# Feed-forward's second product with 512 tokens moving, and another order of units in the attention

## The reference

```python
x = x + attention(layernorm(x))     # 16 heads of 16, softmax over 512 keys
x = x + ffn(layernorm(x))           # out = fwht(silu(x @ W1.T) * (x @ W3.T)) @ W2.T, hidden size 1024
x = x + memory(layernorm(x))        # gated store, scan with decay 0.95 over the tokens, gated load, product
x = x + ffn(layernorm(x))           # the same feed-forward again
```

## Time and profile before

| | us |
|---|---|
| median of 3 runs (564.72 to 565.11) | 565.0 |
| the profiled execution | 566.53 |
| its span | 564.7 |
| PE busy | 552.5 (98%) |
| PEld busy | 383.0 (68%) |
| DVE busy | 382.9 (68%) |
| ACT busy | 311.8 (55%) |
| POOL busy | 178.4 (32%) |

### The profile page before, as it was taken

One profiled execution on the slowest core, in us unless ns is written; L12 is line 12 of the kernel. 1 busy time (PEld: TensorE's weight loads), 2 busy tenths in 40 slices (PEclk: granted clock), 3 DMA queues, 4 the chain that ended last, 5 costly groups with the idle time before them and its releaser, 6 DMA issues.

```text
span 564.7 us, 8930 instructions
## 1 busy us (share of the span) xinstructions
PE 552.5 (98%) x3220; PEld 383.0 (68%) x3220; DVE 382.9 (68%) x729; ACT 311.8 (55%) x581; POOL 178.4 (32%) x209
## 2 busy tenths in 40 slices
PE   8999999999999998999999999999999999999997
PEld 4543343344434433468888888888888888988887
DVE  6988888898898899836465545746886437363333
ACT  3668889876987797743233223366775333323231
POOL 5794467562546242520202002233332010100100
PEclk9989999999999999999999999999999999999999
DMA  7354540231023030021001020110000210112101
GB/s 231 100 180 146 168 132 3 68 128 34 3 94 133 6 147 3 2 74 25 15 7 31 1 38 2 21 18 1 0 2 1 37 39 15 23 38 38 38 1 37
DMA packets 48443, 29.41 MB, mean 52 GB/s; under 512 B 33496, under 2 KB 41688, under 8 KB 48016
## 3 DMA queue, kind: packets, MB, share of 16 engines
q1 hardware_dynamic: 47180, 27.77, 17.1%
q10 hardware_dynamic: 1220, 1.07, 0.7%
HBM read 10.89 MB, written 5.24 MB: 29 GB/s over the span
## 4 chain that ended last, share of the span: by engine, by line
PE 91%; DVE 4%; ACT 2%; issue 1%; DMA 1%; ACTq 0%; POOL 0%; SPq 0%; POOLq 0%
PE PS L392 89%; DVE mxr L1096 2%; PE PS L403 1%; ACT PR L921 1%; PE PS L590 1%; DMA ring<-mT 1%; DMA X<-in_x 1%; DVE OT L1161 0%; ACTq L883 0%; DVE X L1265 0%; DVE X L1178 0%; ACTq L907 0%; DVE bst L1050 0%; PE PS L527 0%; POOL rstd L1338 0%
## 5 line engine op out<-in xcount | busy, mean ns | idle before, releaser
L392 PE MATMUL PS<-xTh,ring 128*128 128x512 f32 x608 | 188.1, 391 | 0.0
L1096 DVE TENSOR_REDUCE mxr<-PS 128x1 f32<-128x512 f32 x256 | 162.9, 680 | 25.5 <-PE PS L392 24.6
L921 ACT ACTIVATE PR<-PS 128x512 f32<-128x512 f32 x256 | 138.0, 602 | 30.3 <-PE PS L392 29.9
L392 PEld LDWEIGHTS PS<-xTh,ring 128*128 128x128 f32 x608 | 113.2, 188 | 23.7 <-issue 1.7
L392 PE MATMUL PS<-xTl,ring 128*128 128x512 f32 x304 | 110.1, 391 | 0.0
L793 ACT ACTIVATE AOh<-PR 128x512 fp32r<-128x512 f32 x72 | 45.5, 632 | 111.4 <-DVE PR L1235 105.9
L392 PE MATMUL PS<-ring 50*128 50x512 f32 (+1 forms) x512 | 100.0, 454 | 4.4 <-DVE mxr L1096 2.8
L1342 POOL TENSOR_TENSOR xTl<-xf,xTh 128x512 fp32r<-128x512 f32 x30 | 42.4, 1428 | 164.9 <-ACT xTh L793 164.9
L1235 DVE TENSOR_TENSOR PR<-PR,PS 128x512 f32<-128x512 f32 x64 | 43.4, 678 | 71.9 <-PE PS L392 51.8
L392 PEld LDWEIGHTS PS<-ring 50*128 50x128 f32 (+1 forms) x512 | 41.6, 185 | 71.1 <-ACT PR L921 43.2
L1088 DVE TENSOR_TENSOR AOl<-PR,AOh 128x512 fp32r<-128x512 f32 x72 | 51.0, 709 | 45.5 <-ACT AOh L793 45.4
(11 more groups left out here) (134 smaller groups left out, 623.6 us busy)
## 6 DMA issues: line engine op xcount, KB each, us to landing
ring<-qh SPq DMA_DIRECT2D x48, 128.0 KB, 2.8
xf<-PR SPq DMA_DIRECT2D x112, 32.0 KB, 1.9
ring<-ql SPq DMA_DIRECT2D x24, 128.0 KB, 2.8
ring<-weight_scratch SPq DMA_DIRECT2D x3, 1024.0 KB, 4.8
weight_scratch<-in_w SPq DMA_DIRECT2D x2, 1024.0 KB, 6.8
X<-in_x SPq DMA_DIRECT2D x3, 512.0 KB, 4.7
out<-X SPq DMA_DIRECT2D x6, 256.0 KB, 2.2
X<-in_w SPq DMA_DIRECT2D x1, 1024.0 KB, 5.5
```

Source lines behind the costliest of these rows:

```text
L392: return nc.tensor.matmul(dst, lhsT, rhs, start=start, stop=stop, skip_group_check=True)
L921: nc.scalar.activation(PR[:, j % 8, :], PS[:, kq_bank(j), :], ACT.Exp, scale=HD ** -0.5)\
L1096: nc.vector.tensor_reduce(mxr[:, S % 2, blk, TT * p + t:TT * p + t + 1], PS[:, QK0 + i % 3, :], AX.X, ALU.max, negate=True).then_inc(max_d ...
```

## The change

1. `down(f)` has a second form for the six chunks of `TURNED = (0, 1, 2, 8, 9, 10)`: the 128 x 128 block of `W2` is stationary and all 512 tokens of the hidden tile move. That is 2 x 3 = 6 matmuls of 512 columns in place of 12 of 256. The result has features in the partitions. So DVE turns the two banks in 32 x 32 blocks into `qf` (`turn_output`), SP puts the blocks in place with 16 DMAs (`output_blocks`, into the idle half of `Vp`), and POOL adds them to `X` (`add_turned`). Chunks 3 and 11 keep the old form; the waits on `x_done` follow, as do the places of the output's stores on SP.
2. The second half of the output projection changes places with the second half of the value projection (`OUT_AT`, `V_AT`), which moves its addition on DVE from step 27 to step 31, and the rounding of the first `AOf` of a batch from ACT's step 28 and POOL's step 29 to step 31 and to step 5 of the next batch.
3. In the last batch the output projection of batch 2 moves from steps 20, 24 and 26 to steps 8, 10, 12 and 14, the last turn of maxima from step 19 to step 20 (behind that step's scores), the split of `W_LIN` from steps 23 to 26 to steps 26 to 29, and the rounding of `AOf` to steps 21 and 22.

```diff
-OUT_AT = ((20,), (24, 26))
-V_AT = ((22,), (28, 30))
-MAX_AT = 3
+OUT_AT = ((20,), (28, 30))
+V_AT = ((22,), (24, 26))
+LAST_OUT_AT = ((8, 10), (12, 14))
+MAX_AT, LAST_MAX_AT = 3, 20
+AO_AT, LAST_AO_AT = STEPS - 1, 21
+TURNED = (0, 1, 2, 8, 9, 10)
...
+            def output_blocks(n):
+                i = TURNED.index(n)
+                sp.wait_ge(y_turned, 2 * i + 2)
+                if i:
+                    sp.wait_ge(x_done, 2 * (TURNED[i - 1] + BATCH + 1))
+                for a in range(4):
+                    for c in range(4):
+                        sp.dma_start(*output_block(a, c)).then_inc(y_in, DMA)
...
             for n in range(BATCH):
                 turned_blocks(n + BATCH + 1)
+                if n in TURNED:
+                    output_blocks(n)
...
 # turn_maxima, PE
                 if s // 8 == 0:
                     pe.wait_ge(x_f, 2 * (b + 1))
-                elif s // 8 < 3 and b < BATCH - 1:
+                elif b == BATCH - 1:
+                    pe.wait_ge(x_done, 2 * b - 2 + s // 8)
+                elif s // 8 < 3:
                     pe.wait_ge(qk_f, 4 * b + 2 * (s // 8))
-                elif s // 8 == 3:
-                    pe.wait_ge(*((x_done, 2 * b) if b else (w2h_done, 3)))
+                else:
+                    pe.wait_ge(*((v_copied, 2 * b + 4) if b else (w2h_done, 3)))
...
 # shared_bank, PE
-                    pe.wait_ge(*((v_copied, 2 * b + 2) if b > 1 else (w2h_done, 4)))
+                    pe.wait_ge(*((x_done, 2 * b - 2) if b > 1 else (w2h_done, 4)))
                     ln_transpose(0, MB)
...
 # down(f), PE
+                    if f == 0 and n - 1 in TURNED:
+                        pe.wait_ge(y_turned, 2 * TURNED.index(n - 1) + 2)
...
+                    if n in TURNED:
+                        for d in range(KD):
+                            ds_ = slice(d * P, (d + 1) * P)
+                            last_ = split_mm(PS[:, 4 + d, :], [(W2l[:, f, ds_], W2h[:, f, ds_], AOl[:, f % 4, :],
+                                                               AOh[:, f % 4, :])], f == 0, f == FT - 1)
+                            if f == FT - 1:
+                                last_.then_inc(y_ready, 1)
+                        return
...
 # ACT's step
-                if s == OUT_AT[1][-1] + 2:
+                if s == (LAST_AO_AT if b == BATCH - 1 else AO_AT):
                     act.wait_ge(aof_ready, 2 * b + 1)
...
 # DVE
-                if b == BATCH - 1 and SPLIT_AT <= s < SPLIT_AT + 8:
-                    w_split_hi((s - SPLIT_AT) // 4, (s - SPLIT_AT) % 4)
+                if b == BATCH - 1:
+                    for w, at in ((W_UP, SPLIT_AT), (W_LIN, 26)):
+                        if at <= s < at + 4:
+                            w_split_hi(w, s - at)
...
+            def turn_output(n):
+                i = TURNED.index(n)
+                if i:
+                    dve.wait_ge(y_in, 16 * DMA * i)
+                for d in range(KD):
+                    dve.wait_ge(y_ready, 2 * n + d + 1)
+                    nc.vector.transpose(qf[:, d, :], PS[:, 4 + d, :]).then_inc(y_turned, 1)
...
 # POOL's step
+                if s == 5 and b:
+                    output_lo(2 * b - 1)
                 if s == 6 and b:
                     output_lo(2 * b)
-                if s == OUT_AT[1][-1] + 3:
+                if s == LAST_AO_AT + 1 and b == BATCH - 1:
                     output_lo(2 * b + 1)
...
+            def add_turned(n):
+                c = n % BATCH
+                pool.wait_ge(y_in, 16 * DMA * (TURNED.index(n) + 1))
+                for k in range(KD):
+                    v = X[:, TT * c:TT * c + TT, k * P:(k + 1) * P]
+                    y = output_sum()[:, k * SEQ:(k + 1) * SEQ].rearrange("p (t u) -> p t u", u=P)
+                    nc.gpsimd.tensor_tensor(v, v, y, ALU.add).then_inc(x_done, 1)
```

More of the change, by code:

```diff
@@ L262, in max_copy, with out_at, turned_at @@
             return ring[r:r + 2, b % 2, QI, 2 * g:2 * g + 2, :].bitcast(F32), mT[16 * blk:16 * blk + 16, :]
+        def out_at(b):
+            return LAST_OUT_AT if b == BATCH - 1 else OUT_AT
+        def turned_at(K):
+            S = (K + LEAD) // 8 - 1
+            if S == LAST_GROUP - 1:
+                return S if K % STEPS == LAST_MAX_AT else None
+            return S if K % 8 == MAX_AT and S < LAST_GROUP else None
         block = ctx.enter_context(nc.Block())
@@ L352, in _ @@
                         weights_in(W_LIN)
[L353 to L356, removed]
+                    S = turned_at(STEPS * b + s)
+                    if S is not None:
+                        max_rows(S)
                     if b == 0 and s == 24:
@@ L376, in _, with store @@
                 turned_blocks(n + BATCH + 1)
+                if n in TURNED:
+                    output_blocks(n)
             ov = out.rearrange("b (t p) d -> b p t d", p=P)
+            def store(c):
+                n = 1 if c == BATCH - 1 else 2
+                for t in range(0, TT, n):
+                    sp.wait_ge(x_done, 2 * (3 * BATCH + c) + (t // n + 1 if n == 1 else 2))
+                    sp.dma_start(ov[c, :, t:t + n, :], X[:, c * TT + t:c * TT + t + n, :]).then_inc(out_done, DMA)
             for c in range(BATCH):
-                n = 1 if c == BATCH - 1 else 2
                 if c < BATCH - 1:
                     turned_blocks(3 * BATCH + 1 + c)
-                for t in range(0, TT, n):
-                    sp.wait_ge(x_done, 2 * (3 * BATCH + c) + t // n + 1)
-                    sp.dma_start(ov[c, :, t:t + n, :], X[:, c * TT + t:c * TT + t + n, :]).then_inc(out_done, DMA)
+                if c:
+                    store(c - 1)
+                if c < BATCH - 1:
+                    output_blocks(2 * BATCH + c)
+            store(BATCH - 1)
             sp.wait_ge(out_done, (2 * BATCH + 2) * DMA)
@@ L624, in shared_bank @@
                         .then_inc(had_ready, 1)
[L625 to L633, removed]
+                for half in range(2):
+                    at = out_at(b)[half]
+                    if b and s in at:
+                        if s == at[0]:
+                            pe.wait_ge(aol_done, 2 * b)
+                            pe.wait_ge(mt_ready, turned)
+                        for part in range(2) if len(at) == 1 else (at.index(s),):
+                            out_projection(half, part)
                 if s == V_AT[0][0] and more:
@@ L659, in _ @@
                     weigh_values((K - 3) // 2)
-                S = (K + LEAD) // 8 - 1
-                if s % 8 == MAX_AT and S < LAST_GROUP:
+                S = turned_at(K)
+                if S is not None:
                     turn_maxima(S, b, s)
@@ L962, in _ @@
                             qk_split(b + 1, n)
-                if s % 8 == MAX_AT and (K + LEAD) // 8 - 1 < LAST_GROUP:
-                    max_evacuate((K + LEAD) // 8 - 1)
+                S = turned_at(K)
+                if S is not None:
+                    max_evacuate(S)
             act.wait_ge(aof_ready, 2 * BATCH)
```

32 lines of the change are left out of this document (24 added, 8 removed).

## The result

| | before | after |
|---|---|---|
| median of the runs, us | 564.86 (564.48 to 565.11) | 569.82 (568.69 to 571.53) |
| ratio after to before | | 1.0078, 95% interval 1.0048 to 1.0108 |
| profiled execution, us (span) | 566.53 (564.7) | 568.69 (566.9) |
| mean granted clock, profiled execution | 0.997 | 0.991 |
| mean granted clock, four runs of after | | 0.991, 0.988, 0.988, 0.985 |

The change makes the kernel 0.8% slower. The forecast was 563.4 with a range of 559.0 to 566.8; all runs of after lie above it. The page says at once that something is new on TensorE: the busy time has hardly moved though 288 matmuls have gone, and the 16th slice (213 to 227 us) has less than the full clock, where before has a 9 from the fourth slice on the earlier trace rows.

The account below looks back on a forecast made before the run. PE was taken to bound both feed-forward rounds and batches 1 and 2, DVE then ACT and PE the last batch. Terms -4.7 + 2.6 + 0.5 = -1.6 on 566.53 gave 564.9, median forecast 563.4, range 559.0 to 566.8 us.

Parts of the forecast that it names:

- The last batch, steps 4 to 18: Batch 3: DVE's wait for POOL delays PE's step 8 by 1.9; with longer pairs the last maximum comes 3.7 us later.
- my rivals: Three alternatives: no wait at step 4 (0.15), last batch's end not shrinking (0.14), second product gaining nothing (0.09).
- The product with 512 tokens: Feed-forward, six chunks: six 512-column matmuls replace twelve of 256 per hidden tile, saving 4.7 us at 0.2265 each.
- third rival: Feed-forward second product gains nothing, 12 short matmuls costing what 6 long ones do; median 568.1, chance 0.09.
- The way back: Feed-forward: DVE's transposes, SP's 16 extra DMAs a chunk and POOL's additions fit beside PE; cost 0.
- Step 4: Batches 1 and 2: DVE's turn into AOf waits 2.0 us for POOL, PE loses 1.6 in each.
- Step 27: Batches 1 and 2: the turn of maxima no longer waits for DVE's output addition, gaining 0.3 in each.
- The last batch, +3.7: Batch 3: the last maximum comes 1.9 + 1.8 = 3.7 us later, from the wait and the longer pairs.
- Behind the last maximum: Last batch, last maximum to last exp: shorter by 2.8 or 3.8 us, middle 3.2 taken.
- second rival: The last batch's stretch behind the last maximum stays 16.8 us, not shrinking; median 566.6, chance 0.14.
- Sum: Whole kernel: -4.7 + 2.6 + 0.5 = -1.6 us on the profiled 566.53, giving 564.9, or 563.4 as median.

Follow-up runs that it names:

- e4: After plus six 128x512 products that nobody reads, added on TensorE at step 5 of batches 1 to 3; 564.9 us.
- e2: Before with the feed-forward part of the change alone; 561.0 us.
- e8: e1 with the last batch put back to before's order (output products, last turn of maxima, rounding); 561.5 us, 560.5 at full clock.
- e3: Before with the attention part of the change alone; 572.9 us.
- e9: Before with one edit: GpSimd forms the rest of AOf's earlier half at step 5 of the next batch, not step 29 of its own; 579.6 us.
- e5: After with GpSimd's rest of AOf's earlier half at step 0, not step 5, in batch 3 alone; 564.8 us.
- e6: After with GpSimd's rest of AOf's earlier half at step 0, not step 5, in batches 1 and 2 alone; 564.9 us.
- e1: After with GpSimd's rest of AOf's earlier half at step 0, not step 5, in batches 1 to 3; 560.7 us.
- e7: e1 with ScalarE's last silu and its rounding placed before the scaling of XNs in chunk 3; 561.5 us.
- e10: After plus three 128x512 products that nobody reads, added on TensorE at step 5 of batches 1 to 3; 567.3 us.

## Why the prediction was wrong

**The step that failed** stands in "The last batch, steps 4 to 18": "PE's step 8 comes 1.9 later", and with it the 1.6 each of batches 1 and 2. That wait itself, its cause, its place and its releaser were right. Its price was taken as a shift of the work behind it at the clock of the earlier trace rows, "granted in full". The price has a second part: PE stands, and behind a stand of that length the clock falls to its lower level. In the profiled execution this is 3.3 us, and e4 shows that it goes when PE is given something to do. All that the clock costs the four runs of after is 4 to 7 us (0.985 to 0.991); that holds falls without a stand too, as the one from 22 to 26 us in the profiled run, and how much of it lies behind stands in the other three no trace shows. None of my rivals had this, so the range ended at 566.8. The trace of before did hold a hint: its clock falls once, near 40 us, which is the one slice with an 8 in the earlier trace rows, and the run of 566.53 lies 1.5 above the median, which is about that fall's price (0.003 of clock, 1.4). I used the 1.5 as a mere offset.

Point by point:

- **The product with 512 tokens, -4.7.** Right. 0.2265 a matmul throughout, 32.64 a chunk, 6 x 0.76 = 4.6. The third rival falls, for both measured forms kept their distances. The Trainium skill's "TensorE: Matmul & The Clock Gate", "Back-to-back issue gap", does not agree with these rows: by its 2.5 ns per matmul the six chunks would have gained 0.7, and they gained 4.6. The Trainium skill's section calls that formula the gap of an isolated matmul, which the prediction left out, and gives about 131 ns for 512 columns in a sustained stream; the rows have 226.5. e2 has the half at 3.9, near 4.6 less chunk 3's 0.4.
- **The way back, cost 0.** Nearly right. The SP queue has the room that I worked out (351.34 + 10.38 = 361.7 against a call at 364.10). ACT still waits 0.60 for the last block and chunk 3 loses 0.4. I have not shown why that block lands late.
- **Step 4, 1.6 in each of batches 1 and 2.** The mechanism was right, the size low: 2.06 and 1.79. PE stands 1.71 and 1.52, near my 1.6. Nearly all of the rest is lost in the same pair of steps: in batch 1 it takes 102.80 - 97.59 = 5.21 us against 100.75 - 97.53 = 3.22 before, 1.99 more. The idle time of a row counts from the end of the matmul before it, which in a stream overlaps the next, so the stand's figure is less than what PE loses.
- **Step 27, -0.3 each.** Right: 0.27 and 0.29.
- **The last batch, +3.7.** The wait of 1.9 was 1.92. The pairs cost some 1.7 against 1.8.
- **Behind the last maximum, -3.2.** 13.0 in place of 13.6: a gain of 3.9 by ACT's own row of work, the upper end (3.8) of what I had worked out, not its middle. With e8's 1.9 for both together the second rival falls.
- **Sum.** Shifts of all terms as measured give about -1.2, my -1.6 was 0.4 off; at full clock the runs have -0.3. The forecast of 563.4 lies 1.1 below the 564.5 of after at full clock; the other 5.3 of the miss of 6.4 us are the clock, with falls behind the stands and falls without one.

## What to carry to other kernels

When a change lets TensorE stand for a microsecond or two in a stretch that was unbroken, the stand's length is the lower end of its price; look for a lower granted clock behind it, and put that price in the range. An instruction of an engine with half its time free can still be the dearest of the change by its place in the order: ask which in-order engine waits for it, and what else that engine has queued. Before reading a difference of under 1%, set the runs beside their mean clock; here that alone separated a change worth 0.3 us from a clock worth 5.

## What the runs showed of the hardware

- Behind stands of TensorE of 1.5 to 1.9 us the granted clock fell to 0.50 for 3.4 us (e3, batch 1) to 13.6 us (e9, batch 3), though the engine was busy again. It fell 1.1 to 2.3 us after the engine had resumed (212.00 and 213.6 in after), and in e9's batch 3 as it resumed. Not behind each of them in each run: in after's profile only behind the third, in e3's behind the first and third, in e5's behind the second, in e6's behind its only one, in e9's behind all three. In the profiles of before, e1, e2, e4, e7, e8 and e10, which have no such stand in batches 1 to 3, the clock is 1.00 there.
- Filling 1.4 us of such a stand with products that serve nothing left half of the runs at clock 1.00 (e4), as often as in kernels without stands, at no cost in time at full clock.
- The same kernel on the same chip has runs with and without such falls. The kernel before took 564.7 us at clock 1.00 and 573.4 at 0.982. In e1's profile the only fall is near 40 us, in the first batch, where TensorE waits 0.39 us for a DMA and 0.27 for an exp. In before's it comes there too, with waits of 0.25 and 0.18, and in e4's, with 0.23 and 0.17, it does not; what decides stays open.
